# The last attention: squares on ScalarE and the queries' half of the finishing on VectorE for every batch

## The reference, cut to what matters

```python
q = (layernorm(x, ln_q_g, ln_q_b) @ Wq + bq)    # [.., 16 heads, 16]
k, v = split(layernorm(x, ln_kv_g, ln_kv_b) @ Wkv + bkv)
q, k = apply_rotary(q * scale, x), apply_rotary(k * scale, x)
qn = layernorm(q, ln_h_g, ln_h_b)               # over the 16 columns of a head
kn = layernorm(k, ln_h_g, ln_h_b)
att = softmax(qn @ kn.T / sqrt(16))             # all 512 keys of the batch
out = (att @ v) @ Wo + bo
```

## Time and profile before

| | us |
|---|---|
| median of 3 runs (2711.46 to 2714.96) | 2713.54 |
| profiled execution | 2709.55 |
| its span | 2707.4 |
| step 0 of the last attention begins, about | 1934 |
| its last batch prepared, about | 2206 |
| its output finished, about | 2307 |

### The profile page before, as it was taken

How to read it: one execution, slowest core, us unless ns; L and a number is a source line. 1 busy time by engine, 2 the same in 40 slices (tenths; PEclk the granted TensorE clock), 3 DMA queues, 4 the chain that set the end, 5 groups by cost and what they waited for, 6 DMA issues and landing times. The chain is left out here.

```text
span 2707.4 us, 41000 instructions
## 1 busy us (share of the span) xinstructions
PE 2346.0 (87%) x12100; PEld 1565.0 (58%) x12100; DVE 1624.5 (60%) x5263; ACT 1299.8 (48%) x3690; POOL 1294.4 (48%) x1301
## 2 busy tenths in 40 slices
PE   5999999996899999999999599992688887699992
PEld 5888888895455555555555456551334343566661
DVE  5767767666766766766776543335766753553334
ACT  3444444444555656656666344432265565343332
POOL 2444545441555555555555158870534310038883
PEclk8999999998999999999999689995799998699996
DMA  5000000011000000000000635553000000515555
GB/s 172 1 16 15 15 15 15 15 52 43 1 1 1 1 1 1 1 1 1 2 1 1 255 63 87 85 80 90 0 0 1 1 1 1 203 36 86 87 85 121
DMA packets 72817, 112.25 MB, mean 41 GB/s; under 512 B 11504, under 2 KB 59632, under 8 KB 72240
## 3 DMA queue, kind: packets, MB, share of 16 engines
q0 software_dynamic: 30336, 42.73, 10.1%
q1 hardware_dynamic: 42304, 67.34, 7.2%
HBM read 80.69 MB, written 36.32 MB: 43 GB/s over the span
## 5 line engine op out<-in xcount | busy, mean ns | idle before, releaser
L1221 POOL TENSOR_TENSOR b_sm<-b_sm,b_rden 128x128 f32<-128x128 f32 (+3 forms) x512 | 355.0, 720 | 355.5 <-DVE b_rden L1174 355.4
L1114 ACT ACTIVATE b_sm<-b_sm,b_mn 128x128 f32<-128x128 f32 (+3 forms) x512 | 284.8, 568 | 22.9 <-DVE b_mn L1166 21.6
L1105 ACT ACTIVATE b_pt<-b_t 128x128 f32<-128x128 f32 (+3 forms) x512 | 195.2, 438 | 143.1 <-PE b_t L1043 143.0
L1166 DVE CUSTOM_DVE_ANT_0 b_sm<-b_f,maskB 128x128 f32<-128x128 f32 (+3 forms) x512 | 233.5, 489 | 2.8 <-issue 1.7
L1033 PE MATMUL b_f<-b_k,b_q 64*128 64x128 f32 (+3 forms) x1024 | 209.6, 485 | 28.9 <-DVE b_prod L1155 14.5
L1155 DVE SCALAR_TENSOR_TENSOR b_prod<-b_f,b_sin 32x512 f32<-32x512 f32 x320 | 219.8, 687 | 4.3
L1590 POOL DMA_INDIRECT XN<-rows,m_slots x158 | 157.7, 998 | 94.0 <-issue 47.5
L2195 ACT ACTIVATE c_pt<-c_second 128x512 f32<-128x512 f32 x256 | 139.2, 598 | 123.6 <-PE c_second L2061 123.3
L2310 DVE TENSOR_REDUCE c_nm<-c_first 128x2 f32<-128x1024 f32 x128 | 155.1, 1220 | 69.8 <-PE c_first L2048 69.8
L1043 PE MATMUL b_t<-ident,b_sm 128*128 128x128 f32 x1280 | 193.2, 281 | 1.1 <-ACT b_pt L1105 0.8
L1043 PEld LDWEIGHTS b_t<-ident,b_sm 128*128 128x128 f32 x1280 | 142.2, 141 | 87.5 <-issue 60.3
(11 more groups left out here) (325 smaller groups left out, 5341.7 us busy)
## 6 DMA issues: line engine op xcount, KB each, us to landing
WM<-in_m_w_dram SPq DMA_DIRECT2D x4, 3072.0 KB, 17.2
WM<-in_m_w_dram SPq DMA_DIRECT2D x4, 2432.0 KB, 14.6
acc<-in_zeros_dram SPq DMA_DIRECT2D x3, 2176.0 KB, 15.2
n_part<-acc SPq DMA_DIRECT2D x12, 512.0 KB, 7.7
a_wa<-in_a_wa_dram SPq DMA_DIRECT2D x8, 512.0 KB, 4.3
b_w<-in_b_w_dram SPq DMA_DIRECT2D x1, 3072.0 KB, 10.3
XN<-rows,m_slots POOLq DMA_INDIRECT x158
X<-in_x_dram SPq DMA_DIRECT2D x4, 512.0 KB, 5.7
```

Of the source, the lines that this page charges most:

```text
L1105: act.activation(pt[:, M % 2, head, 0:t + 1, t * P:(t + 1) * P], back_bank(("t", S, head))[:, 0:keys(t)].rearrange("p (k n) -> p k n", n=P ...
L1114: act.activation(sm[:, s, 0:keys(t)], sm[:, s, 0:keys(t)], ACT.Exp, scale=-1.0, bias=mn[:, s:s + 1], accum_out=den[:, s:s + 1]).then_inc(s ...
L1166: dve.tensor_tensor_reduce(sm[:, s, 0:keys(t)], front_bank(("s", S, head))[:, 0:keys(t)], mask[:, SEQ - keys(t):SEQ], 1.0, -3 * NEG, ALU.a ...
L1221: pool.tensor_tensor(sm[:, s, 0:keys(t)], sm[:, s, 0:keys(t)], rden[:, s:s + 1].to_broadcast([P, keys(t)]), ALU.mult).then_inc(s_pn, 1)
```

## The change

For all batches, not for batch 0 alone: ScalarE squares (GpSimd's `square` is gone), VectorE scales the queries' 256 columns, applies their gain and bias (`finish_q`) and writes their low part (`low_q`), and GpSimd keeps the keys' 256 columns alone. The waits follow: ScalarE's `high` waits for `s_nq` in each batch, the first turn of the queries and `read_qk` wait for `s_lq` of their own tiles, and the reciprocal also waits for `s_scq` of the batch before.

```diff
@@ tensor
-                            pe.wait_ge(s_lq, TB)
+                            pe.wait_ge(s_lq, grp + 4)
@@ scalar, high and square, and the steps
-                    if b == 0:
-                        act.wait_ge(s_nq, n + 1)
+                    act.wait_ge(s_nq, n + 1)
...
-                    act.activation(sq[:, :], qk[:, n, :], ACT.Square).then_inc(s_sq, 1)
+                    act.activation(sq[:, :], qk[:, n % TB, :], ACT.Square).then_inc(s_sq, 1)
...
-                    if tile_at(s, 6, 3) is not None and b == 0:
+                    if tile_at(s, 6, 3) is not None:
                         square(tile_at(s, 6, 3))
@@ vector
-                        dve.wait_ge(s_lq, TB)
+                        dve.wait_ge(s_lq, n - TB + 1)
...
                         dve.wait_ge(s_scaled, b * TB)
+                        dve.wait_ge(s_scq, b * TB)
...
-                    dve.wait_ge(s_rs, 1)
-                    dve.tensor_tensor(x, x, rstd[:, n, 0:C_HEADS]...
+                    dve.wait_ge(s_rs, n // TB + 1)
+                    dve.tensor_tensor(x, x, rstd[:, t, 0:C_HEADS]...
...
                 def low_q(n):
+                    b, t = n // TB, n % TB
                     dve.wait_ge(s_hi, n + 1)
-                    dve.tensor_tensor(stack_q[0][:, n, ...
+                    dve.tensor_tensor(stack_q[b % 2][:, t, ...
...
-                    if tile_at(s, 18, 2) is not None and b == 0:
+                    if tile_at(s, 18, 2) is not None:
                         finish_q(tile_at(s, 18, 2))
-                    if tile_at(s, 20, 2) is not None and b == 0:
+                    if tile_at(s, 20, 2) is not None:
                         low_q(tile_at(s, 20, 2))
@@ gpsimd
-                def square(n):
-                    ...
-                    own = slice(DIM if n < TB else 0, W2)
+                    own = slice(DIM, W2)
...
-                    first = 1 if n < TB else 0
+                    first = 1
...
-                    for i, (stack, at, place) in enumerate(((stack_q[b % 2], t, 2), (stack_k, n % 2, 1))):
-                        if i == 0 and b == 0:
-                            continue
-                        ...
+                    src = heads(qk[:, t, DIM:W2])
+                    x = pool.tensor_tensor(stack_k[:, n % 2, :, C_HD:2 * C_HD].bitcast(F32R), src, stack_k[:, n % 2, :, 0:C_HD],
+                                           ALU.subtract)
...
-                    if tile_at(s, 6, 3) is not None and s >= 0:
-                        square(tile_at(s, 6, 3))
```

More of the change, by code:

```diff
@@ L2288, in inverse @@
                         dve.wait_ge(s_scaled, b * TB)
+                        dve.wait_ge(s_scq, b * TB)
                     dve.reciprocal(rstd[:, :, :], std[:, :, :]).then_inc(s_rs, 1)
                 def finish_q(n):
-                    x, q = heads(qk[:, n, 0:DIM]), qk[:, n, 0:DIM].rearrange("p (h n) -> p h n", n=C_HD)
-                    dve.wait_ge(s_rs, 1)
-                    dve.tensor_tensor(x, x, rstd[:, n, 0:C_HEADS].rearrange("p (h o) -> p h o", o=1).to_broadcast([P, C_HEADS, C_HD]),
+                    t = n % TB
+                    x, q = heads(qk[:, t, 0:DIM]), qk[:, t, 0:DIM].rearrange("p (h n) -> p h n", n=C_HD)
+                    dve.wait_ge(s_rs, n // TB + 1)
+                    dve.tensor_tensor(x, x, rstd[:, t, 0:C_HEADS].rearrange("p (h o) -> p h o", o=1).to_broadcast([P, C_HEADS, C_HD]),
                                       ALU.mult).then_inc(s_scq, 1)
@@ L2302, in low_q @@
                 def low_q(n):
+                    b, t = n // TB, n % TB
                     dve.wait_ge(s_hi, n + 1)
-                    dve.tensor_tensor(stack_q[0][:, n, :, 2 * C_HD:3 * C_HD].bitcast(F32R), heads(qk[:, n, 0:DIM]),
-                                      stack_q[0][:, n, :, 0:C_HD], ALU.subtract).then_inc(s_lq, 1)
+                    dve.tensor_tensor(stack_q[b % 2][:, t, :, 2 * C_HD:3 * C_HD].bitcast(F32R), heads(qk[:, t, 0:DIM]),
+                                      stack_q[b % 2][:, t, :, 0:C_HD], ALU.subtract).then_inc(s_lq, 1)
                 def maximum(f):
@@ L2406, in rotate @@
                     pool.tensor_tensor(qk[:, n % TB, :], pa, pb_, ALU.add).then_inc(s_r, 1)
-                def square(n):
-                    pool.wait_ge(s_cen, n + 1)
-                    pool.wait_ge(s_ssq, n)
-                    pool.tensor_tensor(sq[:, :], qk[:, n % TB, :], qk[:, n % TB, :], ALU.mult).then_inc(s_sq, 1)
                 def scale(n):
                     t = n % TB
-                    own = slice(DIM if n < TB else 0, W2)
+                    own = slice(DIM, W2)
                     pool.wait_ge(s_rs, n // TB + 1)
@@ L2430, in low @@
                     pool.wait_ge(s_hi, n + 1)
-                    for i, (stack, at, place) in enumerate(((stack_q[b % 2], t, 2), (stack_k, n % 2, 1))):
-                        if i == 0 and b == 0:
-                            continue
-                        src = heads(qk[:, t, i * DIM:(i + 1) * DIM])
-                        x = pool.tensor_tensor(stack[:, at, :, place * C_HD:(place + 1) * C_HD].bitcast(F32R), src,
-                                               stack[:, at, :, 0:C_HD], ALU.subtract)
+                    src = heads(qk[:, t, DIM:W2])
+                    x = pool.tensor_tensor(stack_k[:, n % 2, :, C_HD:2 * C_HD].bitcast(F32R), src, stack_k[:, n % 2, :, 0:C_HD],
+                                           ALU.subtract)
                     x.then_inc(s_lo, 1)
```

## The result

The changed kernel took 2718.15 us (median of 9 runs, 2716.91 to 2725.77) against 2713.54 (9 runs, 2709.94 to 2715.72): ratio 1.0024, 95% interval 1.0015 to 1.0034, so 6.5 us slower. (The ratios here are taken over all runs; the two medians alone differ by 4.6 us.) Run again beside other kernels it was 1.0042 (1.0028 to 1.0057), 11.4 us slower. The forecast was 11.4 us. Its profiled execution has a span of 2716.2 us, 8.8 more than before.

What follows compares the result with a forecast made beforehand. No engine was a plain bound; rings of waits among TensorE, VectorE and ScalarE were. Finishing 9.9 plus squares 1.4 gave 11.3 us on 2709.55, 2720.9 profiled, 2725 as run median; range for 8 in 10: 2713 to 2741.

Steps and rivals of the forecast that it cites:

- Sign, and nothing of worth on GpSimd: Last attention, batches 1 to 3: kernel gets slower; work taken off GpSimd is worth 0, since nobody waits for it.
- The verdict: Whole kernel: slower than 2719.0 us 0.83, within 2708.1 to 2719.0 us 0.12, faster 0.05.
- the slack rival: The low part's wait eats only VectorE's gaps: 0 to 5 us, 2713 to 2718 us; chance 0.12.
- The low part's wait: VectorE at step 20 + 2n waits for ScalarE's high copies: 2.1 us at step 20, 1.8 at step 24.
- Its way to TensorE: Steps 18 to 26: late maxima delay TensorE's scores and key turns, reaching +3.7 us; finishing 9.9 us over three batches.
- the queries' chain at step 18: VectorE's scaling, gain and bias precede the values' bias, delaying TensorE's next values projection 0.46 us; hidden in batch 1.
- Sum 1.4 us: ScalarE's squares: 0.6 us at step 12 for each of two batches, 0.2 in batch 1; bounds 0 and 5.7.
- The chain beside GpSimd: VectorE's scaling, gain and bias per tile: 1.34 us undisturbed, 2.59 beside GpSimd, 1.9 taken for the first chain.
- dearer waits: Rival: chains collide with GpSimd and squares are exposed, 2733 to 2745 us; chance 0.16.
- table swaps: Rival: ScalarE's Square evicts the exponentials' table, 9 squares cost 23 us more, 2748 us; chance 0.02.
- faster: Rival: keys' turns at steps 20 to 29 wait for GpSimd's chain, so halving it gives 2707 us; chance 0.05.
- the Square row: Trace before the change: a Square at 1550.82 us follows an Exp with no table load between, against a skill page's rule.

Runs made afterwards that it cites:

- low part back: Changed kernel with the queries' low part of batches 1 to 3 back on GpSimd: ratio 1.0010 to the kernel before.
- low part later: Changed kernel with VectorE's low part of the queries one step later, behind that step's maximum: ratio 1.0038 to the kernel before, +5.7 us at equal clock.
- two moves: Changed kernel with the low part at step 21 and the values' bias ahead of the reciprocal and the queries' chain: ratio 0.9990 to the kernel before.
- squares alone: Kernel before with only the squares of batches 1 to 3 moved to ScalarE: ratio 1.0020, +3.5 us at equal clock.

## Why the prediction was right, step by step

- **Sign, and nothing of worth on GpSimd:** right. GpSimd's busy time in the second stretch fell from 34.9 to 23.2 us, its wait for ScalarE's copies grew to 55.0 us, and no stretch got shorter.
- **The verdict:** "slower, over 2719.0" had a chance of 0.83, and the median came out at 2718.15, just under that line and at the border between the forecast and the slack rival (2713 to 2718). That the kernel is slower is clear from the interval of the ratio and from the second measurement, not from this median.
- **The low part's wait:** right. 2.1, none and 1.8 us were worked out for the first three tiles of batch 3, and the prediction's times give about 3.4 for the fourth; the trace shows 2.23, none, 1.99 and 3.47. Taking the wait away took most of the cost (low part back; low part later, at equal clock only) or, with the values' bias moved too, all of it (two moves); adding it alone brought it.
- **Its way to TensorE:** right in place. Counted from the scores of step 18 (6.44 us late already), the scores of steps 20, 23, 24 and 26 and the first keys' turn come 1.5, 1.8, 4.6, 5.9 and 3.2 us later; forecast were 0.46, 0.75, 2.4, 3.7 and 2.3. Taken apart, two waits for the low part put in 1.7 us before the keys' turn and 1.3 before step 26, 3.0 in all where 3.2 was forecast. The other 2.9 us are the clock: 1.5 at steps 18 and 19 (transposes 1.97 for 1.09, scores 0.79 for 0.50, projection 1.49 for 1.13) and 1.3 at step 23 (transposes 1.94 for 1.09, the four of the output 1.06 for 0.60). The 0.46 us forecast for the queries' chain at step 18 did not show, being covered by the slow transposes, as the prediction had said of batch 1 alone.
- **The step that failed in size is the squares'.** "Sum 1.4 us" counted TensorE's wait alone. The wait was right (0.52 us for 0.6), and so was that only step 12 counts, but the squares alone cost 5.4 us, 3.5 at equal clock, with a lower clock beside them. Within the changed kernel they cannot be told so clearly: with and without them it is 10.0 and 7.4 us at equal clock, a difference of 2.6, with 2.0 either way.
- **The chain beside GpSimd:** the value taken was near enough. The scaling took 508 ns and gain or bias 577 in the mean, 1.66 us a tile for the three by busy time (batch 0's tiles included), against 1.34 and 1.9 taken.
- **Slack swallows it, dearer waits, table swaps, faster:** none came. There is no added table load, so the trace stays with the Square row; and the step-wise delays leave no room for the slack rival.
- **The total** of 11.4 us stands against 6.5 and 11.4 measured, and 10 at equal clock. The agreement is partly luck. The sum was of waits, 11.3 us of them, and TensorE's idle time in the stretches grew by only 7.5. The clock, which the sum put at nothing without a reason, cost 5.8 us of busy time in the stretches (0.8 + 1.8 + 3.2) and gave 3.5 back in the drain; 1.1 more were gained ahead of the first cut, where the kernels do the same work. Within rounding that is the 8.8 us between the profiled spans.

What stays open is why the clock falls where it does. With nothing else changed, the lower clock came with the square of step 12 and went with it (0.91 against 0.96 and 0.98). But the same square and the same wait of 0.52 us stand in the kernel with two moves, at 0.96 and 0.98; and the changed kernel, with more idle time, kept 0.95 where the one with the low part later had 0.91. Each of these figures is of one profiled execution, except the changed kernel's, which came out as 0.95 twice.

## What to carry to other kernels

Before moving work to an engine, look not at how busy it is but at what will be queued behind each new wait: twelve instructions of 0.6 us that waited 27 us in all, in front of the one that frees a PSUM bank pair, cost 9 us at equal clock, while 7 to 8 us of added work in each stretch that held no such wait cost nothing that could be measured. If a moved instruction must wait, put it behind the release that others need, by a step; here that, together with the values' bias moved ahead of another wait, made the whole move free. And read TensorE's busy and idle time of a stretch apart, since the granted clock can add to a small change several times its own wait, or hide it.

## What the runs showed of the hardware

- The same program varied by 13 us along with the mean granted clock: 2706.8 us at 0.939 and 2719.8 at 0.932 for the kernel before.
- Half a microsecond of ScalarE's time in the wrong step went with a mean clock of 0.91 instead of 0.96 and 0.98 over the two stretches, and 4.8 and 6.2 us more of TensorE's busy time; with that one square moved both were back to 0.1 us. In the kernel with two moves the same half microsecond went with 0.96 and 0.98.
- VectorE's instructions with two SBUF inputs, 128x256 in f32, took 0.41 us alone and up to 0.95 beside GpSimd's, and GpSimd's low part 0.97 us instead of 0.73 when VectorE's ran at its start.
